# Router's second product with stationary weights in column strips, logits turned by one transpose

## The chip, the cores and the metric

The kernel runs on one core of a Trainium2 chip. The metric is the device time of one execution in microseconds, and of several runs the median. Data are float32, apart from a few small bf16 tiles that count tokens.

## What is computed

128 sequences of 128 tokens with 256 channels go through a cross attention with a linear (prefix sum) kernel of 16 heads, and then through a feed-forward block in which a router picks one of 8 experts for each token:

```python
# attention, after layernorm of x; ctx is the second input
qp = elu(q) + 1; kp = elu(k) + 1           # q = norm(x) @ Wq + bq, k, v from ctx
res[t] = sum over s <= t of (qp[t] . kp[s]) v[s]
x = x + (res / cumsum(qp)) @ Wo + bo
# router and experts, after layernorm of the new x
h = relu(n @ W1 + b1)                      # 256 -> 128
logits = h @ W2 + b2                       # 128 -> 8
e = argmax(softmax(logits))                # the first of equal ones
x = x + n @ expert_W[e] + expert_b[e]
```

The change concerns `logits`, and how the argmax reads them.

## The kernel before

The work goes in two stages. In the first, 32 groups of four tiles (a tile is one sequence of 128 tokens) pass through a software pipeline of six steps: `load`, `norm`, `project`, `attend`, `merge`, `route`. The step functions of the engines are called 37 times, each time with up to six groups at different stages; a group that is merged in one call is routed in the next. Every engine runs its instructions in the order in which they are written, and semaphores couple them, so the order in each step function is the order of the work. In the second stage 136 slots of up to 128 tokens of one expert each are loaded, transposed, multiplied and stored. The change touches only the first stage and its preparations.

What a call does at the end, on each engine:

TensorE (`step` from line 881): products of keys and queries (`late_scores`, `early_scores`, L822 and L835) into `b_s`; key and value projections (L808, L813); transposes of `xn` (L803); transposes of `x2n` (L803), which wait for ScalarE to have copied the transposed `xn` away (`xnT`); weighted sums of values (`late_sums` L845 in 128x32 strips, `early_sums` L855 in 64x32), among which the query projection and the router's first product stand; then `logit_products` (L861 to L865), the output projection in two halves (`tokens_first`, L813 from `attT`; half b waits for half b of `attT`) and last `ranks` (L867), which counts for each token its place in its expert's bucket. It waits for `onehot`.

`logit_products` takes, for each of the four tiles, the 128x128 block of `hT` as stationary operand and the 8 columns of `w2_sb` as moving one. The result has tokens on partitions, 8 columns a tile, in `b_s`. In float32 each product, and each projection, is issued as two instructions; a transpose is one.

VectorE (`step` from line 594): at the beginning of a call, for the group in `merge`, the two halves of `row` (L601, output projection plus residual), for the group in `route` the places (`ranked` L608, `place` L614), then masks of scores (`masked`, L581), statistics of `row`, `kp` in two halves (L633, L641) with a mask between, values, a mask, `u` (L658), the scan `z` (L664), statistics of the next `x_in`, the first half of `qp` (L591), `attT` in two halves (L681), then the picking of experts for the group in `merge` (L689 to L704: add the bias, maximum, equality, times index, minimum, `onehot`; six small operations, each waiting for the one before), and last the second half of `qp` (L591).

GpSimd (`step` from line 403): for `route`, the count `onehots` (L407) and four indirect DMAs that scatter `row` into `buckets` (L409), all after `place`; for `merge` the row statistics `ve`, `row` (power), `nr` (L422), `row` (L425); for `attend`, `z` times `u` (L431) and the bias added to `x_res` (L433), which waits for the load of `x_res`; for `load` the statistics of `x_in`.

ScalarE (`step` from line 482): exponentials of keys, the normalised `x2n` (L494, waits for GpSimd's L425), `xnT` (L501), `x2T` (L506), queries (L479), `hT` (L513), the second half of the queries, then logarithm and exponential for `u` (L520, L522), then `xn`.

SyncE (`step` from line 312): the load of `x_in`, of `ctxT`, of `x_res`, then, once both halves of `qp` are done, eight small copies of `qp` into `qsel` (L338).

## Time and profile before

| what | value |
|---|---|
| three runs | 1189.24, 1189.86 and 1193.06 us |
| median | 1189.86 us |
| span of the profiled execution | 1158.5 us |
| TensorE busy | 1044.3 us (90%) |
| VectorE busy | 843.8 us (73%) |
| ScalarE busy | 562.7 us (49%) |
| GpSimd busy | 587.0 us (51%) |
| instructions | 39374 |

The profile's span runs from the first to the last instruction; the time of a run also holds what lies around it. The total time of the profiled execution itself is not recorded apart from its span; between the span and the median of the runs lie 31.4 us. Busy time of TensorE is modelled, and a busy engine isn't one at its peak, so the timelines tell more than the shares. In a timeline an entry starts at the time in the first column, takes that in the second, and the bracket tells how long its engine stood idle before it and what released it; entries of one line that follow each other are one row, with their count. The attention stage lasts until about 945 us.

### The profile page before, as it was taken

The page shows a single profiled execution, that of the slowest core. Times are in us where ns is not written, and L with a number is a line of the kernel's source. Part 1 is how long each engine was busy: PE and PEld are TensorE (multiplying, and loading weights), DVE is VectorE, ACT ScalarE, POOL GpSimd, SP SyncE. Part 2 cuts the span into 40 slices and gives each one's busy share as a digit, 9 for nine tenths or more (in the row PEclk, how much of TensorE's full clock was granted, in tenths as well). Part 3 has the DMA queues.
Part 4 walks back from the last instruction along what each step waited for, and adds up shares of the span by engine and source line. Part 5 has one row for each costly group of instructions (what it writes and reads, how often), then busy time and mean ns, then how long its engine had stood idle before and what let it go on. Part 6 is the DMA issues. An engine that isn't in the chain of part 4 may idle for free.

```text
span 1158.5 us, 39374 instructions
## 1 busy us (share of the span) xinstructions
PE 1044.3 (90%) x15828; PEld 727.5 (63%) x15829; DVE 843.8 (73%) x1739; ACT 562.7 (49%) x945; POOL 587.0 (51%) x682
## 2 busy tenths in 40 slices
PE   2989999999999999999999999999999626999996
PEld 1666666666666666666667666666667414666664
DVE  2688887887888887878878788888877643555554
ACT  2544544454555544554455545445444114666664
POOL 4144444544444455554555444544444444777766
PEclk9989999999999999999999999999999857999999
DMA  3823333333333333333334333333322014666664
GB/s 104 241 75 93 94 93 94 93 93 93 94 93 95 97 97 97 101 101 100 107 104 120 97 93 93 93 93 93 93 76 76 30 51 138 193 190 184 195 185 135
DMA packets 88601, 127.11 MB, mean 110 GB/s; under 512 B 13693, under 2 KB 67584, under 8 KB 88320
## 3 DMA queue, kind: packets, MB, share of 16 engines
q1 hardware_dynamic: 75392, 89.98, 30.1%
q0 software_dynamic: 13056, 34.90, 7.9%
q8 instruction: 119, 1.95, 0.7%
q14 instruction: 34, 0.28, 0.1%
HBM read 73.03 MB, written 36.06 MB: 94 GB/s over the span
## 4 chain that ended last, share of the span: by engine, by line
PE 23%; issue 23%; POOL 18%; DMA 13%; SPq 7%; ACT 5%; DVE 4%; DVEq 0%; POOLq 0%; ACTq 0%
DMA x_res<-in_x 8%; PE b_a L808 8%; POOL buckets L409 7%; PE b_b L1014 6%; SPq L338 5%; POOL x_res L433 3%; DMA stage<-buckets 2%; DMA out<-stage 2%; PE b_b L855 2%; PE b_a L1005 2%; ACT x2n L494 2%; POOL row L419 2%; PE b_a L803 2%; PE b_b L813 2%; ACT x2T L506 1%
## 5 line engine op out<-in xcount | busy, mean ns | idle before, releaser
L581 DVE TENSOR_TENSOR stage<-b_s,causal 128x1024 f32<-128x1024 f32 x192 | 226.1, 1219 | 47.6 <-PE b_s L835 37.1
L461 POOL DMA_INDIRECT out<-stage x136 | 136.6, 1005 | 59.2 <-issue 30.2
L409 POOL DMA_INDIRECT buckets<-row,place x128 | 140.8, 1100 | 34.6 <-issue 34.6
L1014 PE MATMUL b_b<-we_sb,x3T 128*128 x544 | 150.5, 400 | 0.0
L808 PE MATMUL b_a<-xnT,wq_sb 128*128 128x512 f32 x256 | 128.0, 624 | 7.4 <-ACT x2T L506 5.1
L539 ACT ACTIVATE x3n<-stage 128x256 f32<-128x256 f32 x136 | 81.5, 599 | 88.4 <-DMA stage<-buckets 83.8
L813 PE MATMUL b_b<-wo_sb,attT 128*128 128x256 f32 x512 | 121.4, 391 | 2.4 <-DVE attT L681 2.4
L494 ACT ACTIVATE x2n<-row 128x256 f32<-128x256 f32 x128 | 66.5, 590 | 115.5 <-POOL row L425 115.5
L407 POOL TENSOR_TENSOR onehots<-onehots,onehot 128x32 bf16<-128x32 bf16 x32 | 7.8, 244 | 223.6 <-DVE place L614 223.6
L808 PE MATMUL b_a<-ctxT,wk_sb 128*128 128x512 f32 x256 | 118.4, 605 | 1.8 <-ACT pos L480 1.8
L813 PE MATMUL b_b<-wv_sb,ctxT 128*128 128x256 f32 x512 | 119.0, 385 | 0.0
L479 ACT ACTIVATE ex<-b_a,bias_q 128x512 f32<-128x512 f32 x64 | 44.0, 688 | 135.8 <-PE b_a L808 135.8
L438 POOL TENSOR_TENSOR ve<-mv,eps_col 128x4 f32<-128x4 f32 x32 | 16.0, 500 | 178.4 <-DVE mv L722 178.4
L813 PEld LDWEIGHTS b_b<-wo_sb,attT 128*128 128x128 f32 x512 | 96.9, 194 | 15.0 <-DVE attT L681 2.6
L1014 PEld LDWEIGHTS b_b<-we_sb,x3T 128*128 128x128 f32 x544 | 93.4, 191 | 20.3 <-issue 5.2
L788 DVE TENSOR_TENSOR stage<-b_b,stage 128x256 f32<-128x256 f32 x136 | 57.8, 425 | 64.5 <-PE b_b L1014 63.5
L813 PEld LDWEIGHTS b_b<-wv_sb,ctxT 128*128 128x128 f32 x512 | 94.7, 190 | 15.8 <-issue 0.5
L433 POOL TENSOR_TENSOR x_res<-x_res,bias_o 128x1024 f32<-128x1024 f32 x32 | 76.5, 2392 | 38.2 <-DMA x_res<-in_x 38.2
L681 DVE TENSOR_TENSOR attT<-b_b,u 128x512 f32<-128x512 f32 x64 | 41.2, 686 | 71.7 <-PE b_b L855 71.7
L487 ACT ACTIVATE ex<-b_a,bias_k 128x512 f32<-128x512 f32 x64 | 44.0, 687 | 87.4 <-PE b_a L808 87.4
L1005 PE MATMUL b_a<-ident,x3n 128*128 128x128 f32 x272 | 56.1, 289 | 31.1 <-ACT x3n L539 24.9
L822 PEld LDWEIGHTS b_s<-qsel,kp 32*128 32x128 f32 x2048 | 62.9, 186 | 28.4 <-issue 27.4
(119 smaller groups left out, 1954.4 us busy)
## 6 DMA issues: line engine op xcount, KB each, us to landing
stage<-buckets SPq DMA_DIRECT2D x136, 130.0 KB, 2.2
x_in<-in_x SPq DMA_DIRECT2D x32, 512.0 KB, 5.1
ctxT<-in_ctx SPq DMA_DIRECT2D x32, 512.0 KB, 6.3
qsel<-qp SPq DMA_DIRECT2D x256, 64.0 KB
x_res<-in_x SPq DMA_DIRECT2D x32, 512.0 KB, 7.3
out<-stage POOLq DMA_INDIRECT x136
we_sb<-in_L_ffn_expert_W SPq DMA_DIRECT2D x8, 256.0 KB, 6.0
buckets<-row,place POOLq DMA_INDIRECT x128
```

Source lines behind the costliest of these rows:

```text
L338: sp.dma_start(qsel[rows, slot(norm), :, s, :], qp[rows, :, :])\
L409: pool.indirect_dma_start(buckets, bass.IndirectOffsetOnAxis(place[:, slot(route), t:t + 1], 0), row[:, slot(route), t, :], None).then_inc ...
L433: pool.tensor_tensor(x_res[:, slot(attend), :, :], x_res[:, slot(attend), :, :], bias_o[:, :].rearrange("p (o n) -> p o n", o=1).to_broadc ...
L461: pool.indirect_dma_start(out.rearrange("t p n -> (t p) n"), bass.IndirectOffsetOnAxis(rows2[:, r, TOKEN:TOKEN + 1].bitcast(U32), 0), sums ...
L494: act.activation(x2n[:, t, :], row[:, slot(merge), t, 0:D], ACT.Identity, bias=row[:, slot(merge), t, SHIFT:SHIFT + 1], scale=row[:, slot( ...
L539: act.activation(x3n[:, load[1] % 2, :], rows2[:, r, 0:D], ACT.Identity, bias=rows2[:, r, SHIFT:SHIFT + 1], scale=rows2[:, r, RSTD:RSTD + ...
L581: dve.tensor_tensor(dst.rearrange("p g h s q -> p g (h s) q"), b_s[:, :, 256 * t:256 * t + 256].rearrange("p g (a q) -> p g a q", q=C), ca ...
L808: last = pe.matmul(dst, w[:, k, P * h:P * h + P], rows[:, k, :], start=(k == 0), stop=(k == KC - 1))
L813: last = pe.matmul(dst, lhsT[:, k, P * t:P * t + P], w[:, k, :], start=(k == 0), stop=(k == KC - 1))
L822: last = pe.matmul(b_s[:, g, 256 * t + 128 * h:256 * t + 128 * h + 128], kp[strip(g), a, h, at:at + P], qsel[strip(g), a, h, :, at + C:at ...
L1005: last = pe.transpose(b_a[:, h, P * k:P * k + P], x3n[:, h, P * k:P * k + P], ident[:, :])
L1014: last = pe.matmul(b_b[:, h, 0:D], x3T[:, h, P * k:P * k + P], we_sb[:, k, bass.ds(e, 1), :], start=(k == 0), stop=(k == KC - 1))
```

## The change

The router's second product has its operands exchanged. The weights `w2` (128x8) are copied once into a 128x32 tile `w2_wide`, zero beyond column 8, and are the stationary operand; the 128 columns of `hT` of each tile are the moving one. The four tiles' results go to four strips of 32 partitions of one bank of `b_s` (columns 0 to 127), so they have experts on partitions and tokens on columns. ScalarE then evicts this 128x128 block with the bias added (`bias_2` is now one column, with `b2` in rows 0 to 7 of every strip, loaded by four small DMAs after the experts' weights) into `logitsT`. TensorE turns it by one transpose into columns 128 to 255 of the same bank, between the two halves of the output projection. VectorE reads the logits from there for the maximum and the comparison; its own addition of the bias is gone, so five small operations are left of six. New tiles: `w2_wide`, `logitsT`; new semaphores: `s_w2` (the copy of the weights), `s_lgT` (evicted), `s_lgTp` (transposed). The declarations of these are left out below.

```diff
@@ -35,10 +35,10 @@
     SLOTS = TILES + E
     STAGES = 6
     RING = 8
-    WEIGHTS = 16 * 14
-    EXPERTS = 16 * (E + 1)
+    WEIGHTS = 16 * 13
+    EXPERTS = 16 * (E + 1 + GT)
     POOL_MADE = 22
-    MADE = 12
+    MADE = 14
     FILL_STEPS = E + 3 + 3 * (E - 1) + 4
 
     with ExitStack() as stack:
@@ -77,7 +77,7 @@
         bias_v = sb("bias_v", [P, D])
         bias_o = sb("bias_o", [P, D])
         bias_1 = sb("bias_1", [FF, 1])
-        bias_2 = sb("bias_2", [P, E])
+        bias_2 = sb("bias_2", [P, 1])
         bias_e = sb("bias_e", [P, E, D])
         wq_sb = sb("wq_sb", [P, KC, D])
         wk_sb = sb("wk_sb", [P, KC, D])
@@ -296,7 +301,7 @@
                     for k in range(KC):
                         sp.dma_start(dst[:, k:k + 1],
                                      b[P * k:P * k + P].rearrange("(p o) -> p o", o=1)).then_inc(s_wld, 16)
-                for dst, b, wide in ((bias_v, bv, D), (bias_o, bo, D), (bias_2, b2, E)):
+                for dst, b, wide in ((bias_v, bv, D), (bias_o, bo, D)):
                     sp.dma_start(dst[:, :],
                                  b.rearrange("(o n) -> o n", o=1).to_broadcast((P, wide))).then_inc(s_wld, 16)
                 sp.dma_start(bias_1[:, :], b1.rearrange("(n o) -> n o", o=1)).then_inc(s_wld, 16)
@@ -306,6 +311,9 @@
                     sp.dma_start(we_sb[:, :, e, :], we[e, :, :].rearrange("(k p) n -> p k n", p=P)).then_inc(s_eld, 16)
                 sp.dma_start(bias_e[:, :, :],
                              be.rearrange("(o e) n -> o e n", o=1).to_broadcast((P, E, D))).then_inc(s_eld, 16)
+                sp.wait_ge(s_cst, MADE)
+                for t in range(GT):
+                    sp.dma_start(bias_2[R * t:R * t + E, :], b2.rearrange("(n o) -> n o", o=1)).then_inc(s_eld, 16)
                 sp.wait_ge(s_const, POOL_MADE)
                 sp.dma_start(buckets[SPARE:SPARE + P, :], pad_row[:, :]).then_inc(s_spare, 16)
 
@@ -513,6 +521,13 @@
                     act.activation(hT[:, :], b_a[0:FF, 1, :], ACT.Relu, bias=bias_1[:, :]).then_inc(s_hT, 1)
                 if norm:
                     first_queries(norm, 1)
+                if merge:
+                    act.wait_ge(s_lg, n(merge, k=1))
+                    if group_no(merge) == 0:
+                        act.wait_ge(s_eld, EXPERTS)
+                    else:
+                        act.wait_ge(s_lgTp, n(merge))
+                    act.activation(logitsT[:, :], b_s[:, 0, 0:P], ACT.Identity, bias=bias_2[:, :]).then_inc(s_lgT, 1)
                 if project:
                     act.wait_ge(s_z, n(project, k=1))
                     if group_no(project) >= 1:
@@ -565,8 +580,11 @@
                                   ALU.add, ALU.mult).then_inc(s_cst, 1)
             dve.memset(expert_of[:, 0:2], 0).then_inc(s_cst, 1)
             dve.memset(slot_e[:, :], 0.0).then_inc(s_cst, 1)
+            dve.memset(bias_2[:, :], 0.0).then_inc(s_cst, 1)
+            dve.memset(w2_wide[:, :], 0.0).then_inc(s_cst, 1)
             dve.wait_ge(s_cst, MADE)
             dve.wait_ge(s_wld, WEIGHTS)
+            dve.tensor_copy(w2_wide[:, 0:E], w2_sb[:, :]).then_inc(s_w2, 1)
 
             def of_mask(which):
                 return causal[:, which, :].rearrange("p (o q) -> p o q", o=1)
@@ -684,21 +702,18 @@
                                           ALU.mult).then_inc(s_att, 1)
                 if merge:
                     if group_no(merge) >= 1:
-                        dve.wait_ge(s_pick, n(merge, 5))
-                    dve.wait_ge(s_lg, n(merge, k=1))
-                    dve.tensor_tensor(logits[:, :, :], b_s[:, 0, 0:GT * E].rearrange("p (t e) -> p t e", e=E),
-                                      per_expert(bias_2[:, :]), ALU.add).then_inc(s_pick, 1)
-                    dve.wait_ge(s_pick, n(merge, 5, 1))
-                    dve.tensor_reduce(top[:, :], logits[:, :, :], axis=AX.X, op=ALU.max).then_inc(s_pick, 1)
-                    dve.wait_ge(s_pick, n(merge, 5, 2))
-                    dve.tensor_tensor(tied[:, :, :], logits[:, :, :], per_tile(top[:, :]), ALU.is_equal)\
-                        .then_inc(s_pick, 1)
-                    dve.wait_ge(s_pick, n(merge, 5, 3))
+                        dve.wait_ge(s_pick, n(merge, 4))
+                    dve.wait_ge(s_lgTp, n(merge, k=1))
+                    scored = b_s[:, 0, P:2 * P].rearrange("p (t e) -> p t e", e=R)[:, :, 0:E]
+                    dve.tensor_reduce(top[:, :], scored, axis=AX.X, op=ALU.max).then_inc(s_pick, 1)
+                    dve.wait_ge(s_pick, n(merge, 4, 1))
+                    dve.tensor_tensor(tied[:, :, :], scored, per_tile(top[:, :]), ALU.is_equal).then_inc(s_pick, 1)
+                    dve.wait_ge(s_pick, n(merge, 4, 2))
                     dve.tensor_tensor(logits[:, :, :], tied[:, :, :], per_expert(iota_m8[:, :]), ALU.mult)\
                         .then_inc(s_pick, 1)
-                    dve.wait_ge(s_pick, n(merge, 5, 4))
+                    dve.wait_ge(s_pick, n(merge, 4, 3))
                     dve.tensor_reduce(first[:, :], logits[:, :, :], axis=AX.X, op=ALU.min).then_inc(s_pick, 1)
-                    dve.wait_ge(s_pick, n(merge, 5, 5))
+                    dve.wait_ge(s_pick, n(merge, 4, 4))
                     if group_no(merge) >= 1:
                         dve.wait_ge(s_hots, n(merge))
                     dve.tensor_tensor(onehot[:, :, :], per_expert(iota_m8[:, :]), per_tile(first[:, :]), ALU.is_equal)\
@@ -793,6 +808,7 @@
         def _(pe):
             pe.wait_ge(s_const, POOL_MADE)
             pe.wait_ge(s_wld, WEIGHTS)
+            pe.wait_ge(s_w2, 1)
 
             def strip(g):
                 return slice(R * g, R * g + R)
@@ -860,7 +876,7 @@
 
             def logit_products():
                 for t in range(GT):
-                    last = pe.matmul(b_s[:, 0, E * t:E * t + E], hT[:, P * t:P * t + P], w2_sb[:, :],
+                    last = pe.matmul(b_s[strip(t), 0, 0:P], w2_wide[:, :], hT[:, P * t:P * t + P],
                                      start=True, stop=True)
                 return last
 
@@ -963,12 +979,15 @@
                     else:
                         pe.wait_ge(s_mc, n(merge, 2, 2))
                     logit_products().then_inc(s_lg, 1)
-                if attend:
-                    for b in range(2):
+                for b in range(2):
+                    if attend:
                         pe.wait_ge(s_att, n(attend, 2, 1 + b))
                         for t in range(b, GT, 2):
                             last = tokens_first(b_b[:, b, D * (t // 2):D * (t // 2) + D], attT, wo_sb, t)
                         last.then_inc(s_y, 1)
+                    if merge and b == 0:
+                        pe.wait_ge(s_lgT, n(merge, k=1))
+                        pe.transpose(b_s[:, 0, P:2 * P], logitsT[:, :], ident[:, :]).then_inc(s_lgTp, 1)
                 if merge:
                     pe.wait_ge(s_hot, n(merge, k=1))
                     if group_no(merge) >= 1:
```

## Rows read from the trace of the kernel before

**Rows 1.** Timeline of TensorE (PE); columns: start us, us, engine, line, operation, output, input, count [idle before, releaser].
```profile
420.89 1.10 PE L845 MATMUL b_b<-stage,vsel 128*32 128x64 f32 x64
...
427.40 1.05 PE L863 MATMUL b_s<-w_sb,hT 128*128 128x8 f32 x8
428.30 3.70 PE L813 MATMUL b_b<-wo_sb,attT 128*128 128x256 f32 x16
...
444.59 1.06 PE L803 MATMUL b_a<-ident,x2n 128*128 128x128 f32 x8 [0.87 <-ACT xnT L501]
...
472.42 1.06 PE L803 MATMUL b_a<-ident,x2n 128*128 128x128 f32 x8 [0.86 <-ACT xnT L501]
```

**Rows 2.** Line 803: duration min/median/max in ns; idle time before it, us, times.
```profile
L803 PE MATMUL b_a<-ident,x2n x256: 272/273/475, 83.4 to 933.6; 128*128 128x128 f32 x128
...
  ACT xnT L501: 22.4, 26
```

**Rows 3.** Timeline of VectorE (DVE) in the same group.
```profile
427.50 1.29 DVE L681 TENSOR_TENSOR attT<-b_b,u 128x512 f32<-128x512 f32 x2 [1.25 <-PE b_b L855]
428.70 0.18 DVE L689 TENSOR_TENSOR logits<-b_s,bias 128x32 f32<-128x32 f32 x1
...
429.92 0.68 DVE L591 SCALAR_TENSOR_TENSOR qp<-ex,pos 128x512 f32<-128x512 f32 x1
430.52 0.68 DVE L601 TENSOR_TENSOR row<-b_b,x_res 128x512 f32<-128x512 f32 x1
432.04 0.69 DVE L601 TENSOR_TENSOR row<-b_b,x_res 128x512 f32<-128x512 f32 x1 [0.83 <-PE b_b L813]
432.65 0.18 DVE L608 TENSOR_TENSOR ranked<-b_a,onehot 128x32 f32<-128x32 f32 x1
432.93 0.19 DVE L614 TENSOR_REDUCE place<-ranked 128x4 uint32<-128x32 f32 x1
433.46 2.36 DVE L581 TENSOR_TENSOR stage<-b_s,causal 128x1024 f32<-128x1024 f32 x2 [0.34 <-PE b_s L822]
...
437.53 0.66 DVE L633 SCALAR_TENSOR_TENSOR kp<-ex,pos 128x512 f32<-128x512 f32 x1
...
440.40 0.68 DVE L641 SCALAR_TENSOR_TENSOR kp<-ex,pos 128x512 f32<-128x512 f32 x1
```

**Rows 4.** Timeline of GpSimd (POOL) in the same group.
```profile
433.20 0.24 POOL L407 TENSOR_TENSOR onehots<-onehots,onehot 128x32 bf16<-128x32 bf16 x1 [5.53 <-DVE place L614]
...
437.52 1.49 POOL L409 DMA_INDIRECT buckets<-row,place  x1 [0.30 <-issue]
...
440.46 0.68 POOL L422 TENSOR_TENSOR nr<-row,neg_one 128x4 f32<-128x4 f32 x1
```

**Rows 5.** Timeline of ScalarE (ACT) in the same group.
```profile
443.44 1.00 ACT L501 ACTIVATE xnT<-b_a 128x1024 f32<-128x1024 f32 x1
```

**Rows 6.** Timelines of VectorE and TensorE in the last group that attends.
```profile
916.95 1.29 DVE L681 TENSOR_TENSOR attT<-b_b,u 128x512 f32<-128x512 f32 x2 [3.52 <-PE b_b L855]
...
917.69 3.72 PE L813 MATMUL b_b<-wo_sb,attT 128*128 128x256 f32 x16
...
919.83 0.69 DVE L601 TENSOR_TENSOR row<-b_b,x_res 128x512 f32<-128x512 f32 x1 [0.37 <-PE b_b L813]
```

**Rows 7.** Timelines of TensorE and GpSimd in one of the two shorter groups.
```profile
122.83 3.70 PE L813 MATMUL b_b<-wo_sb,attT 128*128 128x256 f32 x16
...
134.38 0.20 POOL L422 TENSOR_TENSOR nr<-row,neg_one 128x4 f32<-128x4 f32 x1
...
149.88 3.70 PE L813 MATMUL b_b<-wo_sb,attT 128*128 128x256 f32 x16
```

**Rows 8.** Timeline of GpSimd in the group whose projection starts at 539.67.
```profile
549.25 1.14 POOL L409 DMA_INDIRECT buckets<-row,place  x1 [0.31 <-issue]
```

**Rows 9.** Timelines of GpSimd and VectorE in the group whose projection starts at 400.45.
```profile
417.82 2.37 POOL L433 TENSOR_TENSOR x_res<-x_res,bias_o 128x1024 f32<-128x1024 f32 x1 [1.80 <-DMA x_res<-in_x]
...
418.18 3.09 DVE L658 SCALAR_TENSOR_TENSOR u<-z,u 128x1024 f32<-128x1024 f32 x1
```

More of the change, by code:

```diff
@@ L87, in build @@
         w2_sb = sb("w2_sb", [FF, E])
+        w2_wide = sb("w2_wide", [FF, R])
         we_sb = sb("we_sb", [P, KC, E, D])
@@ L117, in build @@
         hT = sb("hT", [FF, N])
+        logitsT = sb("logitsT", [P, P])
         logits = sb("logits", [P, GT, E])
@@ L203, in build @@
         s_hT = sem("s_hT")
+        s_w2 = sem("s_w2")
         s_lg = sem("s_lg")
+        s_lgT = sem("s_lgT")
+        s_lgTp = sem("s_lgTp")
         s_pick = sem("s_pick")
```

## The prediction

> **What bounds the kernel now.** I read the timeline of TensorE through one group in the middle of the attention stage first, then what TensorE's transposes wait for, then VectorE, GpSimd and ScalarE in the same stretch. Times in a group are told from T, the start of its output projection (L813 from `attT`); in the group of the rows T is 428.30. The transposes of `x2n` start at 444.59 and again at 472.42, so a group takes 27.83 us; TensorE works all of it but for 0.87 us, in which it waits for ScalarE's `xnT` [rows 1]. That wait stands in 26 groups and sums to 22.4 us [rows 2]. So the engine looks full, but a chain through the other engines ends last: TensorE's output projection, VectorE's second `row` addition (L601) at 432.04, `ranked` and `place` at 432.93 [rows 3], GpSimd's four scatters and the row statistics up to `nr` (L422) [rows 4], ScalarE's `x2n`, then `xnT` at 443.44, which ends 0.15 us before the transposes start [rows 5].
>
> One link of this chain is odd, and it decides the sum. The fourth scatter starts at 437.52, within 0.01 us of VectorE's `kp` (L633), and takes 1.49 us; `nr` starts at 440.46, 0.06 after the second `kp` (L641), and takes 0.68, ending 0.06 after it [rows 3, 4]. In one group (T = 122.83) `nr` comes at T + 11.55, not at T + 12.16, and takes 0.20 us: neither it nor the scatter ahead of it was held, and the next group starts after 149.88 - 122.83 = 27.05 us, not 27.83 [rows 4, 7]. In another it starts 0.36 us later than usual (549.25, T being 539.67) and takes only 1.14 us, ending at 10.72 after T as always (437.52 + 1.49 - 428.30 = 10.71) [rows 4, 8]. So GpSimd is held while `kp` runs, and what releases the chain is the end of VectorE's second `kp`: a later `place` is swallowed by these stalls, a later `kp` is not. The Trainium skill, SBUF — State Buffer, "Who interferes with whom", says that a VectorE instruction with two SBUF inputs contends with a GpSimd instruction that reads SBUF. By that rule `nr` stalls, and the trace agrees (0.68 us against 0.20). The same section infers that a `tensor_tensor` leaves descriptor generation alone; the fourth scatter's 1.49 us speaks against carrying that over to `kp`, and I go by the trace.
>
> **The change, part by part.** *Logit products.* Before: 8 instructions with 128-column weights, 427.40 to 428.30, 0.90 us [rows 1]. After: 8 with 32-column weights and 128 moving columns in four column strips. The nearest row in strips is L845: 64 instructions of 64 columns in 1.10 us, 17 ns each [rows 1]; twice the columns gives 34 ns, 0.28 us for 8. The other end is the old rate, 0.90 us, plus a change of array shape. I take 0.3, for the shape is that of L845. But the saving has no taker: the output projection needs the first half of `attT`, which starts at 427.50 and one half of which takes 0.68 us; in the last group, where the pair begins at 916.95, the projection starts at 917.69, 0.06 after the first half's end [rows 3, 6]. So T can move from 428.30 to 428.18 + 0.06 = 428.24, and with 0.02 for the cold weight load to 428.26: a gain of 0.04 us where 0.6 were saved; its bounds are 0.06 and, at the old rate with a change of shape of 0.2, a loss of 0.2. The Trainium skill, TensorEngine Tiling (Array Packing), "Key Properties", says that changing the tiling mode drains TensorE. By it the change adds one drain, before the projection; it would lie in the same 0.5 us of waiting, and nothing in the sum moves.
>
> *Eviction on ScalarE.* One 128x128 activation, between 0 and the 1.00 us of the eight times larger `xnT` [rows 5]. It starts after the products and must end before half the projection, 1.8 us after T: hidden. It adds no semaphore wait on ScalarE that outlasts the old one for `attT`.
>
> *The transpose.* One more instruction of TensorE: the 8 transposes of `x2n` take 1.06 with one of 0.27 at the end, so 0.11 us a slot [rows 1, 2]. TensorE's own work later in the group moves by that: +0.11.
>
> *What VectorE now waits for.* This is the price. Before, its picking began at 428.70, right behind `attT`, T + 0.40 [rows 3]. Now its first reduction waits for the transpose, which stands behind half the output projection. Earliest: 8 slots of (3.70 - 0.38)/15 = 0.22 us after T, plus 0.27 and 0.03 of hand-over, T + 2.07 [rows 1, 2]. Latest: in the group with T = 917.69 VectorE had waited for that same half and began at 919.83, T + 2.14 [rows 6]; with the slot of 0.11 that is T + 2.25. I take 2.20, since the second end is a measured hand-over. Behind this wait are queued five small operations (the first of the six goes; 429.92 - 428.70 - 0.22 = 1.00 us), `qp` (0.60), the first `row` addition (0.60): the second `row` addition starts at T + 4.40 instead of 432.04, T + 3.74. Its wait of 0.83 for TensorE is used up. `ranked` follows 0.61 later, `place` 0.28 after that (T + 5.29), and the mask of the scores (L581) some 0.11 later, T + 5.40. Before it began at 433.46, T + 5.16, after 0.34 us of waiting [rows 3]. VectorE is thus 0.24 us late, `place` 0.66.
>
> *What comes of it.* `kp` shifts from T + 9.23 to 9.47 and ends near 10.13; the fourth scatter arrives at T + 9.22 + 0.66 = 9.88, is held till then and ends at about 10.96; `nr` arrives 0.06 after the second `kp` as before and is released at its end. The chain is late by VectorE's 0.24, not by `place`'s 0.66. With the 0.04 gained at T this is 0.20 us a group. Bounds: with T + 2.07, VectorE is 0.11 late and so is TensorE, 0.07 net; with T + 2.25 and no gain at T, 0.29.
>
> *The queue of SyncE.* The second `qp` ends 1.4 us later (T + 3.8), and the eight `qsel` issues, the loads of `x_in`, `ctxT` and `x_res` stand behind it. `x_res` is the one that matters: GpSimd adds to it at 417.82 (T + 17.37, T being 400.45) after waiting for it, and VectorE's `u` then takes 3.09 us [rows 9]. In the new order GpSimd gets there about 1.4 us later and may meet `u` or the scan. After the slower `u` VectorE still idles 1.25 us before the next `attT` [rows 3, 9]; the collision moved to the scan costs up to 0.6 more of that. I count nothing; if the cover went, each 0.1 us would cost 3 us in all.
>
> *Start and tail.* One broadcast load of a bias fewer, four small ones and a copy of 128x8 more, all beside longer loads: 0. For the last two groups with scatters there is no `kp` to hide `place`; they pay the whole 0.66 - 0.04 = 0.62.
>
> **The sum.** 28 groups x 0.20 = 5.6. The group of 27.05 us [rows 7] and one other like it lived on a scatter ahead of `kp`; with `place` later they fall back: 2 x 0.78 = 1.6. Tail 2 x 0.62 = 1.2. Together +8.4. The profiled span goes from 1158.5 to 1166.9; 31.4 us lie between the span and the median of the three runs, whose own spread is 3.8, and I leave them as they are: 1189.86 + 8.4 = 1198.3. With the bounds of the wait: 28 x 0.07 + 2.8 = 4.8 and 28 x 0.29 + 2.8 = 10.9, so 1194.7 to 1200.8.
>
> **The rivals.** (a) The chain is late by all of `place`: the stalls don't swallow it, say because the second scatter or the statistics meet `kp` elsewhere. For: everything from `place` to `xnT` is serial. Against: the group with the late scatter [rows 8]. Price 0.62 x 30 + 1.6 = 20, 1210. (b) VectorE's lateness is itself swallowed, because the mask waits for TensorE anyway and the transpose comes earlier than I take it. For: 0.34 us of wait ahead of the mask. Price 0 to 0.07 a group, 1190 to 1193.4. (c) TensorE's own work is the bound and the products' saving counts: (0.90 - 0.30 - 0.11) x 30 = 15 less, 1175. For: it idles only 0.87 in 27.83. Against: the wait for `xnT` and `attT` ending 0.12 before T. (d) Faster by another way: the order of GpSimd and `kp` flips and the 27.05 us of [rows 7] become the rule, 28 x 0.78 = 22 less, plus 0.2 a group: 1173. It decides at 0.06 us, the lead of the second `kp` over `nr`. Against: the scatter now comes 0.4 us after `kp` starts, not beside it. (e) The strips don't overlap and the change of shape costs more than I allow: the products take 1.1 us, T is 0.2 later, 6 us more, 1204.
>
> **How the numbers follow.** Own forecast 0.52, (a) 0.12, (b) 0.20, (c) 0.05, (d) 0.06, (e) 0.05. Likeliest: 1198.3. A measurement of this kernel can tell about 0.3%, 3.6 us. Slower by more: forecast, (a), (e), less the forecast's lowest edge: 0.66. Within: (b), and 0.03 of the forecast: 0.23. Faster: (c) and (d), 0.11. The range leaves out (c), (d) and part of (a): 1189.5 to 1209.
>
> **What would show it.** Right: TensorE shows an idle time ahead of the output projection, released by `attT`, VectorE's first reduction starts near T + 2.2 behind a wait for the transpose, the second `row` addition has no wait, the mask starts near T + 5.4, the fourth scatter takes about 1.1 us, `nr` still 0.68, and a group takes 28.03. Wrong: a period under 27.8 with `nr` at 0.20 (d), one of 28.4 with `nr` unstalled (a), or a projection that starts later than 0.06 after `attT` (e).

## The result, and the profile after

The changed kernel takes 1200.5 us (median of 4 runs, 1198.95 to 1203.71) against 1189.55 for the one before (median of 4 beside it, 1188.46 to 1193.06): a ratio of 1.0097, 95% interval 1.0077 to 1.0118. It is about 1% slower. Forecast were +8.4 us and 1198.3; measured are +10.9 and 1200.5.

One thing must be known before any trace is compared. The runs of this kernel lie on two levels. The first set of runs gives 1189.6 us for the kernel before; three later sets, on three different chips, give 1157.8, 1158.4 and 1157.4. The chip of the first set isn't on record, so a difference between chips is possible. The ratio is the same on both levels (1.0097 above, 1.0090 below, interval 1.0064 to 1.0117). The profile that stands ahead of the prediction, with its span of 1158.5 us, fits the lower level, and the first profile of the changed kernel is from the upper one. There is no profile of the kernel before at the upper level. So I compare the profile before with a second profile of the changed kernel, taken at the lower level, where the two programs took 1157.8 and 1168.2 us. The head of the page of the changed kernel, first at the upper level:

```profile
span 1197.1 us, 39477 instructions
PE 1038.4 (87%) x15860; PEld 717.4 (60%) x15861; DVE 843.9 (70%) x1710; ACT 573.9 (48%) x977; POOL 566.4 (47%) x682
```

and at the lower one:

```profile
span 1164.7 us, 39477 instructions
PE 1034.1 (89%) x15860; PEld 705.7 (61%) x15861; DVE 851.7 (73%) x1710; ACT 572.5 (49%) x977; POOL 582.9 (50%) x682
```

TensorE is busy for 10 us less than before (1044.3 in the table above) and the span is 6.2 longer. The timeline of TensorE in the middle of the attention stage, changed kernel, lower level; it is the counterpart of [rows 1]. T, the start of the output projection, is 428.20:

```profile
427.35 0.42 PE L879 MATMUL b_s<-hT,w_wide 128*32 128x128 f32 x8
428.20 1.99 PE L829 MATMUL b_b<-wo_sb,attT 128*128 128x256 f32 x8 [0.43 <-DVE attT L699]
430.03 0.27 PE L990 MATMUL b_s<-ident,logitsT 128*128 128x128 f32 x1
430.14 1.89 PE L829 MATMUL b_b<-wo_sb,attT 128*128 128x256 f32 x8
...
444.69 1.06 PE L819 MATMUL b_a<-ident,x2n 128*128 128x128 f32 x8 [0.95 <-ACT xnT L509]
...
456.20 1.13 PE L829 MATMUL b_b<-wo_sb,attT 128*128 128x256 f32 x4 [0.43 <-DVE attT L699]
```

The products in strips take 0.42 us where they took 1.05, and the saving stands in the next line as idle time, 0.43 us behind VectorE's `attT`. The transposes of `x2n` still wait for `xnT`, and a little longer. The group takes 456.20 - 428.20 = 28.00 us; in a second profile of the kernel before, from the same set, the usual group takes 27.84.

VectorE and GpSimd in the same group, the counterpart of [rows 3] and [rows 4]:

```profile
427.45 1.29 DVE L699 TENSOR_TENSOR attT<-b_b,u 128x512 f32<-128x512 f32 x2 [1.53 <-PE b_b L871]
430.41 0.19 DVE L708 TENSOR_REDUCE top<-b_s 128x4 f32<-128x32 f32 x1 [1.67 <-PE b_s L990]
...
431.41 0.69 DVE L609 SCALAR_TENSOR_TENSOR qp<-ex,pos 128x512 f32<-128x512 f32 x1
432.02 1.28 DVE L619 TENSOR_TENSOR row<-b_b,x_res 128x512 f32<-128x512 f32 x2
...
433.50 0.18 DVE L632 TENSOR_REDUCE place<-ranked 128x4 uint32<-128x32 f32 x1
433.60 2.36 DVE L599 TENSOR_TENSOR stage<-b_s,causal 128x1024 f32<-128x1024 f32 x2
...
437.67 0.66 DVE L651 SCALAR_TENSOR_TENSOR kp<-ex,pos 128x512 f32<-128x512 f32 x1
...
440.51 0.68 DVE L659 SCALAR_TENSOR_TENSOR kp<-ex,pos 128x512 f32<-128x512 f32 x1
```

```profile
438.09 1.07 POOL L417 DMA_INDIRECT buckets<-row,place  x1 [0.30 <-issue]
...
440.61 0.64 POOL L430 TENSOR_TENSOR nr<-row,neg_one 128x4 f32<-128x4 f32 x1
```

VectorE idles 1.67 us for the transpose, and from there to `kp` it never waits: the two additions of `row` are one row of the timeline, and the mask of the scores follows `place` at once. Both idle times that stood there (0.83 and 0.34, [rows 3]) are used up. `nr` is still held (0.64 us) to the end of the second `kp`.

### The profile page after: what moved, and what is told of

Read it like the earlier page. It is cut to its first block and busy times, and to the rows that moved or that the text cites. A ratio compares the mean times of both kernels' runs of the same rounds, so it can differ in the third digit from the quotient of the medians.

```text
span 1197.1 us, 39477 instructions
## 1 busy us (share of the span) xinstructions
PE 1038.4 (87%) x15860; PEld 717.4 (60%) x15861; DVE 843.9 (70%) x1710; ACT 573.9 (48%) x977; POOL 566.4 (47%) x682
## 5 line engine op out<-in xcount | busy, mean ns | idle before, releaser
L599 DVE TENSOR_TENSOR stage<-b_s,causal 128x1024 f32<-128x1024 f32 x192 | 225.7, 1217 | 60.4 <-remote 56.5
L1033 PE MATMUL b_b<-we_sb,x3T 128*128 x544 | 159.1, 419 | 44.0 <-DVE stage L803 16.4
L469 POOL DMA_INDIRECT out<-stage x136 | 139.2, 1023 | 99.3 <-DVE stage L803 59.1
L417 POOL DMA_INDIRECT buckets<-row,place x128 | 130.8, 1022 | 34.7 <-issue 34.7
L1033 PEld LDWEIGHTS b_b<-we_sb,x3T 128*128 128x128 f32 x544 | 100.6, 206 | 64.5 <-issue 53.9
L803 DVE TENSOR_TENSOR stage<-b_b,stage 128x256 f32<-128x256 f32 x136 | 57.8, 425 | 108.6 <-PE b_b L1033 83.0
L829 PEld LDWEIGHTS b_b<-wo_sb,attT 128*128 128x128 f32 x512 | 92.2, 190 | 36.1 <-DVE attT L699 23.8
L562 ACT ACTIVATE x3T<-b_a 128x256 f32<-128x256 f32 x136 | 51.9, 382 | 90.4 <-PE b_a L1024 54.2
L861 PEld LDWEIGHTS b_b<-stage,vsel 128*32 128x32 f32 x4096 | 60.4, 110 | 37.2 <-issue 25.6
L838 PEld LDWEIGHTS b_s<-qsel,kp 32*128 32x128 f32 x2048 | 62.9, 186 | 28.4 <-issue 27.4
```

The costliest lines, as they stand in the source:

```text
L417: pool.indirect_dma_start(buckets, bass.IndirectOffsetOnAxis(place[:, slot(route), t:t + 1], 0), row[:, slot(route), t, :], None).then_inc ...
L469: pool.indirect_dma_start(out.rearrange("t p n -> (t p) n"), bass.IndirectOffsetOnAxis(rows2[:, r, TOKEN:TOKEN + 1].bitcast(U32), 0), sums ...
L599: dve.tensor_tensor(dst.rearrange("p g h s q -> p g (h s) q"), b_s[:, :, 256 * t:256 * t + 256].rearrange("p g (a q) -> p g a q", q=C), ca ...
L803: dve.tensor_tensor(sums[:, r, :], b_b[:, h, 0:D], sums[:, r, :], ALU.add).then_inc(s_sums, 1)
L829: last = pe.matmul(dst, lhsT[:, k, P * t:P * t + P], w[:, k, :], start=(k == 0), stop=(k == KC - 1))
L838: last = pe.matmul(b_s[:, g, 256 * t + 128 * h:256 * t + 128 * h + 128], kp[strip(g), a, h, at:at + P], qsel[strip(g), a, h, :, at + C:at ...
```

## The experiments

Where a run is told to be some us above the kernel before, its time stands beside runs of that kernel on the same chip. All runs of this section are at the lower level.

**Both kernels again (b_again, a_again).** Unchanged.

> The kernel before, unchanged, to see a second profiled execution of it. Its first profile had a span of 1158.5 us, 31.4 less than the median of its runs, while the profile of the changed kernel lies 2.7 us below its own run. Theory S (the profile of before was an unusually fast execution; the ordinary one has a slower expert stage): this profile has a span near 1186, the last projection count near 944 us as before, and the expert stage behind it takes some 243 us instead of 215. Theory G (the gap is outside the span): the span is 1158 again, with the run at 1189. Ratio of times 1.000.

Measured: 1159.82 us beside 1157.83, ratio 1.0012 (0.9998 to 1.0027); the span is 1157.4. Neither theory holds as written. The expert stage wasn't unusually fast, and there is no 31 us outside the span: the profiled execution took 1159.15 us, 1.75 more than its span. The profile of before most likely belongs to another level than the runs that it was shown with.

> The changed kernel, unchanged, to see whether its profile repeats: second mask pair of VectorE starting 12.04 us after the output projection's start (9.99 before), nr taking 0.20 us instead of 0.68, a period of 27.67 us in the attention stage, 257 us from the count of the tokens to the end. Theory R (these belong to the program): all four again, time near 1200. Theory C (they were chance of one execution): at least the expert stage is another, by over 10 us, at the same time of the run.

Measured: 1168.15 us, ratio 1.0090 (1.0064 to 1.0117). None of the four signs came again, so theory R is refuted: a usual group takes 28.00 us and `nr` 0.64. The expert stage is another, as theory C has it, but the time of the run is another too. The count of the tokens closes the attention stage. Its rows of b_again, of a_again and of the changed kernel at the upper level:

```profile
941.89 0.17 DVE L743 COPY count<-b_s 128x8 f32<-128x8 f32 x1 [0.71 <-PE b_s L985]
```

```profile
948.66 0.17 DVE L758 COPY count<-b_s 128x8 f32<-128x8 f32 x1 [0.71 <-PE b_s L1004]
```

```profile
939.62 0.17 DVE L758 COPY count<-b_s 128x8 f32<-128x8 f32 x1 [0.71 <-PE b_s L1004]
```

From there to the end of the span it is 215.5, 216.0 and 257.5 us. At the lower level the expert stage is the same in both kernels, and the change costs 948.66 - 941.89 = 6.8 us of attention stage. Read across the levels (943.65 us in the profile before, 939.62 in the changed kernel at the upper level), the same change would seem to speed the attention stage up and to slow down by 43 us a stage that it doesn't touch. Such a comparison mixes the change with the level and shows neither. Where the loss arises at the upper level stays open, for want of a partner.

**The expert stage cut away (b_cut, a_cut).** Only 16 of the 136 slots run, so only the rows of these slots are written.

```diff
+    RUN = 16
...
-            with eng.Fori(1, SLOTS // RING, 1) as i:
+            with eng.Fori(1, RUN // RING, 1) as i:
...
-            begin((SLOTS // RING, -2), 2)
+            begin((RUN // RING, -2), 2)
...
```

> The kernel before with the expert stage cut to 16 of its 136 slots, so that only the first rows of the output are written; attention, router, scatters and the slot tables are whole. It gives the attention stage's share in ordinary executions. The cut slots are 120 of 136. If the ordinary expert stage takes 243 us from the count to the end (1187 less 944), some 1.75 us a slot, this kernel takes about 1189.5 - 120 x 1.7 = 985 us; if it takes the 215 us of the first profile (1.37 us a slot), about 1025.

> The changed kernel with the same cut of the expert stage to 16 of 136 slots. Theory P (the sum of the prediction: all of the loss arises in the attention stage, by VectorE's lateness): 8 us above b_cut, or the whole 11 us of the measured loss. Theory E (the profiles compared: attention 4 us faster, the loss arises in the expert stage, whose code isn't changed): 4 us below b_cut, and the remaining 15 us are in the 120 slots cut away.

Measured: 995.67 us (ratio to the whole kernel before 0.8595, interval 0.8572 to 0.8619) and 1004.71 (0.8679, 0.8653 to 0.8704). The two differ by 9.0 us, the whole kernels by 10.3. The 120 slots are worth 162.2 and 163.4 us, 1.35 and 1.36 a slot. For b_cut neither expected time came (985 or 1025): both started from the upper level's 1189.5. From 1157.8 the smaller price, 1.37 a slot, gives 993. Most of the loss arises ahead of the 120 slots, in plain timings; theory E, made from profiles of two levels, is refuted at this one.

**The transpose one tile earlier (a_mid).**

```diff
+            def turn_logits(merge):
+                pe.wait_ge(s_lgT, n(merge, k=1))
+                pe.transpose(b_s[:, 0, P:2 * P], logitsT[:, :], ident[:, :]).then_inc(s_lgTp, 1)
...
                         for t in range(b, GT, 2):
                             last = tokens_first(b_b[:, b, D * (t // 2):D * (t // 2) + D], attT, wo_sb, t)
+                            if merge and t == 0:
+                                turn_logits(merge)
                         last.then_inc(s_y, 1)
-                    if merge and b == 0:
-                        pe.wait_ge(s_lgT, n(merge, k=1))
-                        pe.transpose(b_s[:, 0, P:2 * P], logitsT[:, :], ident[:, :]).then_inc(s_lgTp, 1)
+                    if merge and not attend and b == 0:
+                        turn_logits(merge)
```

> The changed kernel with the transpose of the logits one tile earlier: in the first half of the output projection after one tile's products instead of two. Theory V (VectorE's lateness behind the transpose is what costs): the transpose moves from T + 1.83 to about T + 0.95, VectorE's first reduction from 2.20 to about 1.3, the second row addition waits for TensorE again and starts at T + 3.85 (3.74 of before and a slot of 0.11), the mask at T + 5.27, kp at 9.34; a group takes 27.83 + 0.11 - 0.05 = 27.89 us and the kernel 2 to 3 us more than before instead of 10: ratio 1.002. Theory W (the cost is the transpose, the eviction or the strips by themselves, wherever they stand): a ratio of 1.009 as with the whole change.

Measured: ratio 1.0020 (1.0007 to 1.0034), 1160.87 us beside 1158.4. VectorE in a group with T = 397.66:

```profile
399.00 0.19 DVE L708 TENSOR_REDUCE top<-b_s 128x4 f32<-128x32 f32 x1 [0.80 <-PE b_s L885]
...
401.53 0.69 DVE L619 TENSOR_TENSOR row<-b_b,x_res 128x512 f32<-128x512 f32 x1 [0.23 <-PE b_b L829]
...
402.95 1.23 DVE L599 TENSOR_TENSOR stage<-b_s,causal 128x1024 f32<-128x1024 f32 x1 [0.34 <-PE b_s L838]
```

The first reduction starts at T + 1.34, and both waits for TensorE are back. The same instructions in the same number, one of them one tile earlier, cost 2.5 us instead of 10.3. A usual group takes 27.92, and two groups of 27.1 are there again, as in the kernel before.

**The transpose behind both halves (a_late).**

```diff
-                    if merge and b == 0:
+                    if merge and b == 1:
```

> The changed kernel with the transpose behind both halves of the output projection. VectorE's first reduction moves from T + 2.20 to about 4.0, all its later work by 1.8. Theory V (each tenth of VectorE's lateness counts in full, through kp, nr, x2n and xnT): a group takes 28.05 + 1.8 = 29.85 us, the kernel some 54 us more than the changed one, ratio 1.055. Theory H (the idle times that follow, ahead of the third mask and ahead of attT, take some of it, or nr runs into another place): clearly less than 1 us a group.

Measured: ratio 1.0547 (1.0526 to 1.0568), 1220.54 us. In the group with T = 419.24 the first reduction starts at T + 3.93, 1.72 later than in the changed kernel, and all that follows shifts with it:

```profile
423.17 0.19 DVE L708 TENSOR_REDUCE top<-b_s 128x4 f32<-128x32 f32 x1 [3.39 <-PE b_s L990]
...
437.46 0.74 PE L819 MATMUL b_a<-ident,x2n 128*128 128x128 f32 x5 [1.25 <-ACT xnT L509]
```

The transposes of `x2n` start at T + 18.22 instead of 16.49, 1.73 later, and a group takes 29.73, 1.73 more. VectorE's lateness reaches TensorE one for one.

**GpSimd alone delayed (b_gp).** The kernel before, with a memset of a spare tile ahead of the scatters.

```diff
...
+                    pool.wait_ge(s_hots, n(route, k=1))
+                    pool.memset(idle_a[:, :], 0.0).then_inc(s_idle, 1)
+                    pool.wait_ge(s_idle, n(route, k=1))
                     for t in range(GT):
                         pool.indirect_dma_start(
```

> The kernel before with GpSimd alone delayed: a memset of a spare 128x512 tile, some 0.6 us with its hand-over, stands ahead of the four scatters, so that they are as late as in the changed kernel while VectorE and TensorE are untouched. Theory K (GpSimd is held by kp and the chain is released at the end of the second kp, so that lateness of place is swallowed): the first scatter moves from T + 5.31 to about 5.95, the fourth takes 1.08 instead of 1.50, nr still ends at about T + 12.83, a group still takes 27.83; only the two groups of 27.05 are lost and the tail pays, 2 to 3 us, ratio 1.002. Rival (a) of the prediction (the chain is late by all of it): 0.6 x 30 = 18 us, ratio 1.016.

Measured: ratio 1.0059 (1.0036 to 1.0083), 1164.12 us beside 1157.36, more than theory K gave and far less than rival (a). GpSimd in the group with T = 372.17, and its second `kp`:

```profile
377.37 0.53 POOL L411 MEMSET idle_a<- 128x512 f32 x1
...
382.10 0.96 POOL L414 DMA_INDIRECT buckets<-row,place  x1 [0.30 <-issue]
...
384.51 0.49 POOL L427 TENSOR_TENSOR nr<-row,neg_one 128x4 f32<-128x4 f32 x1
```

```profile
384.26 0.68 DVE L646 SCALAR_TENSOR_TENSOR kp<-ex,pos 128x512 f32<-128x512 f32 x1
```

The scatters come 0.70 us later, the fourth at T + 9.93 is not held at all, `nr` ends 0.06 after the second `kp` as ever, and the usual group takes 27.84 us, to the hundredth what it took without the memset. The 6.8 us come from elsewhere. Beside b_again the trace has no group of 27.05 left (1.6 us), the first interval of the pipeline is 1.5 longer, one is 0.35 longer, the last two together 0.8, and the first projection starts 0.9 later. These make 5.2 us; the rest isn't accounted for. The start and the first interval also differ between executions of one kernel (that interval took 29.8 us in the profile before and 26.85 in b_again), so 2.4 of the 5.2 may be chance.

**The chain through `nr` taken away (b_nr, a_nr).** GpSimd does the row statistics ahead of the last scatter, in the kernel before and in the changed one.

```diff
-                    for t in range(GT):
+                    for t in range(GT - 1):
                         pool.indirect_dma_start(
...
                     pool.tensor_copy(row[:, slot(merge), :, TOKEN].bitcast(U32),
                                      tokens[:, bass.ds(n(merge, GT), GT)]).then_inc(s_token, 1)
+                if route:
+                    pool.indirect_dma_start(
+                        buckets, bass.IndirectOffsetOnAxis(place[:, slot(route), GT - 1:GT], 0),
+                        row[:, slot(route), GT - 1, :], None).then_inc(s_bucket[slot(route)], 16)
```

> The kernel before with GpSimd's row statistics (ve, row, nr, row, tokens) put ahead of the last of the four scatters instead of behind it. If the chain scatters, nr, x2n, xnT ends last, as the prediction has it, taking it away leaves TensorE's own work: nr at about T + 10.7 instead of 12.16, xnT then waits for the transposes of xn alone, the idle time of 0.87 us ahead of the transposes of x2n goes, and a group takes 26.96 us: 0.87 x 30 = 26 us less, ratio 0.977. If another wait stands right behind it (attT, the third mask), less than half of that.

> The changed kernel with the same order of GpSimd as b_nr. With the chain through nr gone, VectorE's 0.24 us a group no longer reach TensorE. Theory N (the chain was the only way by which the change costs): the difference to b_nr is the transpose's 0.11 us a group less what the shorter products give back at T (0.05), so 0 to 3 us, ratio to the kernel before 0.978 to 0.980. Theory M (the lateness reaches TensorE another way too, through the third mask or attT): 6 us or more above b_nr.

Measured: 0.9809 (0.9782 to 0.9837) and 0.9852 (0.9834 to 0.9871), 1133.73 and 1141.66 us. They had been expected at 0.977 and at 0.978 to 0.980. In b_nr `nr` has its 0.20 us and TensorE has no idle time ahead of `x2n` any more; T = 360.02 and the next projection follow:

```profile
371.16 0.20 POOL L422 TENSOR_TENSOR nr<-row,neg_one 128x4 f32<-128x4 f32 x1
```

```profile
375.50 1.07 PE L807 MATMUL b_a<-ident,x2n 128*128 128x128 f32 x8
387.07 1.11 PE L817 MATMUL b_b<-wo_sb,attT 128*128 128x256 f32 x4
```

From the second group to the end of the steady part every one takes 27.05 us, give or take 0.01. So the 27.05 of [rows 7] was TensorE's own limit in this order of work, but for 0.18 us in each group behind ScalarE's `x2T`, and the chain through `nr` was what held all others. In a_nr a usual group takes 27.12: with the chain gone, 0.24 us of lateness on VectorE no longer reach TensorE, and what is left is the transpose's slot less the gain at T (0.11 - 0.05), as theory N has it. The whole kernels differ by more, 7.9 us, which is what theory M gave (6 or more) and not theory N (0 to 3). Besides 1.9 us of usual groups there are 2.3 in four longer ones, 1.9 in the last two, and the first projection starts 2.2 us later. That last share may be chance (in the traces of this study it starts between 62.6 and 66.8 us). The longest of the four, T = 526.95 with 28.01 us, does show a second way from VectorE to TensorE: the second `kp` comes 0.27 us late, meets GpSimd's last scatter and its product of `z` and `u`, and takes 3.60 us instead of 0.68; the weighted sums then wait for the values, `vsel`. VectorE, then TensorE:

```profile
539.53 3.60 DVE L663 SCALAR_TENSOR_TENSOR kp<-ex,pos 128x512 f32<-128x512 f32 x1
```

```profile
544.52 1.25 PE L865 MATMUL b_b<-stage,vsel 128*32 128x64 f32 x64 [0.89 <-DVE vsel L670]
```

Two of the other long groups hold a gap of about 0.5 us in the middle of these sums that has no releaser in the trace. So the chain through `nr` is the way by which the usual group pays, and it isn't the only one in all groups.

**The order in which the change pays (a_ord, b_ord_nr, c_best).** a_ord is the changed kernel with TensorE's tail in another order (shown below) and ScalarE's eviction ahead of the second queries (not shown); c_best has GpSimd's order as well; b_ord_nr is the kernel before, with its old products, in both orders.

```diff
                     early_sums(attend, 0)
-                if norm:
-                    if merge:
-                        pe.wait_ge(s_hT, n(merge, k=1))
-                    channels_first(b_a[:, 1, :], wq_sb, xnT, 1).then_inc(s_q, 1)
                 if attend:
                     early_sums(attend, 1).then_inc(s_o, 1)
...
                     logit_products().then_inc(s_lg, 1)
+                if norm:
+                    if merge:
+                        pe.wait_ge(s_hT, n(merge, k=1))
+                    channels_first(b_a[:, 1, :], wq_sb, xnT, 1).then_inc(s_q, 1)
+                if merge:
+                    pe.wait_ge(s_lgT, n(merge, k=1))
+                    pe.transpose(b_s[:, 0, P:2 * P], logitsT[:, :], ident[:, :]).then_inc(s_lgTp, 1)
...
-                    if merge and b == 0:
-                        pe.wait_ge(s_lgT, n(merge, k=1))
-                        pe.transpose(b_s[:, 0, P:2 * P], logitsT[:, :], ident[:, :]).then_inc(s_lgTp, 1)
```

> The changed kernel with another order: TensorE does both early sums, then the logit products, then the second half of the query projection, then the transpose, then the output projection; ScalarE evicts the logits ahead of the second queries. attT and the eviction now lie beside 2 us of projection, TensorE never waits for them, and VectorE's picking is not behind any part of the output projection. If the shorter products were lost only in the wait for attT and VectorE only late by the transpose's place, a group takes 27.83 - 0.48 + 0.11 = 27.46 us: 11 us less than before, ratio 0.991. If the new form costs by itself, it stays at or above 1.000.

> The kernel before, old logit products, with both orders: row statistics ahead of the last scatter, and early sums, logit products, second half of the query projection, output projection on TensorE. TensorE is the bound (27.05 us a group in b_nr) and its work is the same, so as b_nr: ratio 0.980. It is the partner of the next kernel, from which it differs by the change of the logit products alone.

> The changed kernel with both orders. Where TensorE is the bound and neither attT nor VectorE waits behind the transpose, the change gives what its products save, 1.06 - 0.43 modelled (0.90 - 0.43 to the start of the next) less 0.11 for the transpose: a group takes 27.05 - 0.37 = 26.68 us, 11 us less than b_ord_nr, ratio 0.971. If it gives nothing here either, the strips' saving is an artefact of the modelled ends: ratio 0.980.

Measured: a_ord 0.9817 (0.9791 to 0.9843), b_ord_nr 0.9725 (0.9702 to 0.9749), c_best 0.9637 (0.9608 to 0.9667); 1135.41, 1125.73 and 1116.03 us. TensorE in b_ord_nr, then in c_best:

```profile
352.83 1.48 PE L859 MATMUL b_b<-stage,vsel 64*32 64x64 f32 x128
354.24 1.06 PE L867 MATMUL b_s<-w_sb,hT 128*128 128x8 f32 x8
355.15 1.96 PE L812 MATMUL b_a<-xnT,wq_sb 128*128 128x512 f32 x4
356.95 3.62 PE L817 MATMUL b_b<-wo_sb,attT 128*128 128x256 f32 x16
```

```profile
351.73 1.48 PE L875 MATMUL b_b<-stage,vsel 64*32 64x64 f32 x128
353.14 0.43 PE L883 MATMUL b_s<-hT,w_wide 128*32 128x128 f32 x8
353.50 1.98 PE L828 MATMUL b_a<-xnT,wq_sb 128*128 128x512 f32 x4
355.32 0.27 PE L988 MATMUL b_s<-ident,logitsT 128*128 128x128 f32 x1
355.43 3.62 PE L833 MATMUL b_b<-wo_sb,attT 128*128 128x256 f32 x16
```

From the products to what follows it is 0.91 us in the one and 0.36 in the other; with 0.11 for the transpose the change now saves 0.44 us a group. The usual group takes 26.63 and 26.20, and the kernels differ by 9.7 us. The same products, eviction and transpose that cost 10 us where they were put give 10 back where TensorE is the bound and nothing waits behind the transpose. c_best is 41 us faster than the kernel before.

The order itself brought some 0.4 us a group that I had not counted: b_ord_nr was expected where b_nr is, at 27.05, and a_ord at 27.46 takes 27.00. The early sums, 128 in one run, take 1.48 us where two runs of 64 took 0.86 each, and all from them to the projection takes 4.12 us (352.83 to 356.95) where it took 4.47 in b_nr; the rest, 0.08, is the projection's.

## Why the prediction was right, point by point

All of this part but its last paragraph is about the lower level, where both kernels have a profile.

**The chain, and who releases it.** Right, and now shown: without `nr` behind the scatters the group falls to 27.05 (b_nr), with the scatters alone 0.70 us later it stays at 27.84 (b_gp). Rival (a) is refuted by the second, and a_late shows that lateness of VectorE itself is passed on.

**T and the products.** The strips took 0.42 us, 0.3 were taken. `attT` starts 0.75 before T, where it was 0.80: T moved by 0.05, 0.04 were taken. The 0.02 us for a cold weight load no run shows: the projection starts 0.06 after the first half of `attT`, as in [rows 6]. The saving of 0.6 us waits behind `attT`, as forecast. Rival (c) is refuted for the kernel as changed, and c_best shows where it would have been true. Rival (e) is refuted by the 0.42 us of the products and by this 0.06.

**VectorE's steps.** Taken and measured, from T: first reduction 2.20 and 2.21, second addition without a wait, `place` 5.29 and 5.30, mask 5.40 and 5.40, `kp` 9.47 and 9.47. Of the lateness of 0.24 us 0.21 are left at the second `kp` (12.31 after T, 12.10 before), the transposes of `x2n` are 0.20 later (16.49 against 16.29 in [rows 1]), and the part from there to the next T is 0.05 shorter. So a usual group costs 0.16 us, not 0.20, and `nr` is held at its 0.64 as said.

**What was counted at nothing.** The eviction takes 0.37 us from T - 0.36 on, beside the wait for `attT`. `x_res` is later, as said, and meets `u` or the scan in turn. What covers it is VectorE's idle time ahead of `attT`, first in b_again, then in a_again (groups of the page: busy, mean ns | idle before):

```profile
L681 DVE TENSOR_TENSOR attT<-b_b,u 128x512 f32<-128x512 f32 x64 | 41.2, 686 | 75.7 <-PE b_b L855 75.7
```

```profile
L699 DVE TENSOR_TENSOR attT<-b_b,u 128x512 f32<-128x512 f32 x64 | 41.2, 686 | 57.3 <-PE b_b L871 57.3
```

Of 75.7 us of cover 18.4 are gone, and in the usual group none of it reached TensorE. The usual groups of b_nr and a_nr say the same.

**The two short groups.** Both of 27.05 us in b_again are gone in a_again. But the trade goes both ways: in a_again one group takes 27.55 and one 27.88, because the second mask comes late and `nr` slips ahead of the second `kp`. The first of them, T = 764.96, VectorE and GpSimd:

```profile
775.65 2.35 DVE L599 TENSOR_TENSOR stage<-b_s,causal 128x1024 f32<-128x1024 f32 x2 [0.56 <-PE b_s L838]
777.92 0.68 DVE L659 SCALAR_TENSOR_TENSOR kp<-ex,pos 128x512 f32<-128x512 f32 x1
```

```profile
777.37 0.20 POOL L430 TENSOR_TENSOR nr<-row,neg_one 128x4 f32<-128x4 f32 x1
```

That is rival (d), in one group: VectorE 0.65 us later makes the group 0.45 shorter. It didn't become the rule at this level.

**A term that was missing.** Seven groups of a_again take 0.06 to 0.35 us more than 28.00, 1.9 in sum. They are small hold-ups that a full VectorE passes on; one of them was followed to its source. The same one stands in both traces, `place` starting 0.45 us behind `ranked`'s end, 0.35 later than usual; first in b_again (T = 535.96), then in a_again (T = 175.51):

```profile
540.94 0.19 DVE L614 TENSOR_REDUCE place<-ranked 128x4 uint32<-128x32 f32 x1 [0.46 <-DVE ranked L608]
```

```profile
181.16 0.19 DVE L632 TENSOR_REDUCE place<-ranked 128x4 uint32<-128x32 f32 x1 [0.45 <-DVE ranked L626]
```

Before, the next projection follows after 27.84 us as always: the 0.34 of idle time ahead of the mask takes it up. Afterwards the group takes 28.35.

**A term that was too large.** For the tail 1.2 us were counted. There VectorE has no `qp` ahead of the additions, `place` comes at T + 4.76 instead of 4.62, and the last two groups take 0.3 us more, while the end of the stage behind them is 0.7 shorter.

**The sum.** Forecast: 5.6 for the groups, 1.6 for the short ones, 1.2 for the tail, 8.4. In the traces of one level: 27 groups x 0.16 = 4.3, 1.6 for the two short ones, 1.9 of hold-ups, 0.6 back through the two groups above, 7.2 from the third group to the thirtieth; to the end of the span it is 1164.7 - 1157.4 = 7.3. The medians differ by 10.3. Of the 3 us between, 2 are within what a repetition moves: the kernel before ran at 1157.8 and 1159.8 in one set, and against the second of these the difference is 8.3. The last 1 us lies outside the spans of the two profiled executions (1159.15 and 1167.48 us, 8.3 apart).

**The 31.4 us, and the upper level.** I left them as they were and added the difference to the median. I took them for time that belongs to the profiled execution; it was a trace of another level. The runs of the changed kernel at the upper level, with a span of 1197.1 beside 1199.84 us, show that only 2.7 us lie around a span. So that the difference fits the upper level too is luck. Its trace of the changed kernel even shows the sign that the prediction gave for rival (d): a usual group takes 27.56 us, under 27.8, and `nr` takes 0.20 every time. GpSimd in the group with T = 423.98:

```profile
436.38 0.20 POOL L430 TENSOR_TENSOR nr<-row,neg_one 128x4 f32<-128x4 f32 x1
```

The mechanism of the prediction is thus shown for the lower level, where it gives 7.3 us between the spans. By which way the kernel loses 10.9 us at the upper level, where the forecast was measured, isn't shown.

## What to carry to other kernels

When an operation on the busiest engine is made shorter, ask what its successor waits for: if that is another engine's result, the saving turns into a wait, and the hand-over that was added is the only thing left. An engine's idle time in front of a hand-over is not waste but what swallows the new lateness, once; after it is used up, what comes on top counts in full (in a_late, 1.72 us on VectorE cost 1.73 a group), small hold-ups too. Move the added hand-over behind independent work before judging such a change, and compare two traces only when runs of both programs at the same level stand beside them.

## What the runs showed of the hardware

**How long GpSimd is held.** The fourth scatter takes 0.96 us when `kp` has ended before it starts (b_gp, T + 9.93), 1.07 when `kp` still runs for 0.24 us (changed kernel), 1.49 when both start together [rows 4]. In the two held cases it ends 0.83 us after the end of `kp`. A scatter that starts 0.06 us ahead of `kp` isn't held at all (0.96 us, in the first of the two short groups of b_again). The Trainium skill, SBUF — State Buffer, "Who interferes with whom", says that a VectorE instruction with two SBUF inputs contends with GpSimd where that reads SBUF, and infers that descriptor generation is left alone by `tensor_tensor`; `kp` is a `scalar_tensor_tensor` with two SBUF inputs, and the trace shows that it does hold the scatter (1.07 and 1.49 us against 0.96). The second scatter of a group, beside a mask that reads PSUM and SBUF, takes 0.96. It goes the other way round as well: the second `kp` of a_nr above took 3.60 us.

**Two levels, and a late release.** At the upper level VectorE's steps up to `kp` stand at the same distances from T as at the lower one, and then the second mask doesn't. Changed kernel, first set, T = 423.98:

```profile
433.45 0.66 DVE L651 SCALAR_TENSOR_TENSOR kp<-ex,pos 128x512 f32<-128x512 f32 x1
436.02 2.36 DVE L599 TENSOR_TENSOR stage<-b_s,causal 128x1024 f32<-128x1024 f32 x2 [1.91 <-remote]
438.29 1.57 DVE L659 SCALAR_TENSOR_TENSOR kp<-ex,pos 128x512 f32<-128x512 f32 x1
```

The products that it waits for (L838), and by the kernel's code for nothing else, stand where they do at the lower level, the last one starting near T + 9.6, yet the mask starts at T + 12.04. This happens 30 times, 56.5 us in all; `nr` is then always ahead of the second `kp` and takes 0.20, and the attention stage is 9 us shorter than at the lower level (939.62 against 948.66). In the expert stage the same trace shows the loss of the level: 1.68 us from output to output instead of 1.38, with waits at L803 of up to 4.3 us (13.2 in all) that have no releaser in the trace. Between 100 and 900 us the granted clock of TensorE is 1.00 (2.4 GHz) in both traces of the changed kernel, so it doesn't explain the late mask. From 1000 us on its mean is 0.93 at the upper level and 1.00 at the lower one, where TensorE is busy for 79% and 94% of the time; even if a whole slot were TensorE's time, that would make 1.48 us of 1.38 (an estimate from these two clocks), not 1.68. What delays the release isn't known; no other trace of this study is from that level.
